# One pair more between the mix and the turn of a talking-heads attention: counting of sides, exp and selection two groups later, with nine score buffers

## What is computed

```python
q, k = l2norm(x @ Wq), l2norm(x @ Wk)            # 16 heads of 64; 4 memory keys ahead of k
dots = einsum('bhid,bhjd->bhij', q, k) * 10
dots = einsum('hg,bgij->bhij', W_pre_th, dots)   # heads are mixed
dots = where(causal, mask_value, dots)
vk   = top_k(dots, 64)[..., -1:]                 # the 64th largest of each row
attn = softmax(where(dots < vk, mask_value, dots))
attn = einsum('hg,bgij->bhij', W_post_th, attn)  # heads are mixed again
out  = einsum('bhij,bhjd->bhid', attn, v) * head_scale
out  = (out * sigmoid(x @ Wg + bg)) @ Wo
```

## Time and profile before

| | us |
|---|---|
| median of 3 runs | 2402.39 (2402.37 to 2406.88) |
| the profiled run | 2402.8 |
| its span, first to last instruction | 2401.0 |
| PE busy in the span | 2104.1 (88%) |
| DVE busy | 1801.4 (75%) |
| ACT busy | 1622.8 (68%) |
| POOL busy | 812.5 (34%) |

### The profile page before, as it was taken

One profiled execution on the slowest core, in us unless ns is written; L12 is line 12 of the kernel. 1 busy time (PEld: TensorE's weight loads), 2 busy tenths in 40 slices (PEclk: granted clock), 3 DMA queues, 4 the chain that ended last, 5 costly groups with the idle time before them and its releaser, 6 DMA issues. The chain is left out here.

```text
span 2401.0 us, 55203 instructions
## 1 busy us (share of the span) xinstructions
PE 2104.1 (88%) x16059; PEld 1363.1 (57%) x16060; DVE 1801.4 (75%) x7282; ACT 1622.8 (68%) x4700; POOL 812.5 (34%) x2274
## 2 busy tenths in 40 slices
PE   7995789898999998899989988998898889884997
PEld 3433456665566556665666666666666666563433
DVE  6564489868986898689868986898689868983446
ACT  4442578757876787678767885888588758871543
POOL 3001444344434433443344334433443344311000
PEclk9996899999999999999999999999999999997998
DMA  5002012101210121012101210121012101212001
GB/s 171 0 9 75 22 38 60 42 25 42 59 42 25 42 60 42 25 42 60 42 25 42 60 42 25 42 59 42 25 42 60 42 23 40 57 37 85 0 1 70
DMA packets 113218, 104.71 MB, mean 44 GB/s; under 512 B 34448, under 2 KB 110864, under 8 KB 112912
## 3 DMA queue, kind: packets, MB, share of 16 engines
q1 hardware_dynamic: 108000, 96.65, 15.8%
q10 hardware_dynamic: 4912, 4.46, 0.6%
HBM read 19.14 MB, written 12.71 MB: 13 GB/s over the span
## 5 line engine op out<-in xcount | busy, mean ns | idle before, releaser
L1491 DVE TENSOR_SCALAR_CACHE_REDUCE S<-S,minus_thr 128x68 f32<-128x68 f32 (+56 forms) x456 | 218.0, 514 | 225.6 <-POOL minus_thr L1388 224.8
L1048 PE MATMUL bankC<-R,E 128*128 128x128 f32 x2560 | 349.9, 286 | 34.6 <-POOL R L1395 34.6
L1048 PEld LDWEIGHTS bankC<-R,E 128*128 128x128 f32 x2560 | 337.3, 201 | 70.7 <-POOL R L1395 36.7
L1032 PE MATMUL bankB<-raw,mixpre 128*128 128x76 f32 (+37 forms) x1024 | 357.8, 437 | 19.3 <-DMA raw<-SC 19.2
L1244 ACT ACTIVATE S<-bankB,aim_first 128x68 f32<-128x68 f32 (+56 forms) x456 | 231.2, 510 | 201.5 <-PE bankB L1032 199.7
L1379 POOL TENSOR_TENSOR S<-S,diagmask 128x8 f32<-128x8 f32 x512 | 108.6, 216 | 688.2 <-ACT S L1244 654.7
L1022 PE MATMUL bankD<-KT,QT 64*64 64x258 f32 (+7 forms) x2304 | 195.6, 409 | 94.2 <-ACT SC L1233 86.0
L1395 POOL TENSOR_SCALAR R<-mixpost,rinv 128x128 f32<-128x128 f32 x512 | 184.8, 374 | 180.1 <-DVE rinv L1555 179.7
L1551 DVE SCALAR_TENSOR_TENSOR E<-S,limit,E 128x68 f32<-128x68 f32 (+56 forms) x456 | 221.2, 521 | 30.4 <-DVE E L1551 0.3
L1270 ACT ACTIVATE E<-S,nmax 128x12 f32<-128x12 f32 (+56 forms) x512 | 233.2, 505 | 14.5 <-POOL nmax L1409 14.5
L1074 PEld LDWEIGHTS bankM<-PT,V 128*64 128x64 f32 x5120 | 183.9, 141 | 102.4 <-issue 85.9
(11 more groups left out here) (176 smaller groups left out, 3968.8 us busy)
## 6 DMA issues: line engine op xcount, KB each, us to landing
X_first<-in_L_attn_x_dram ACTq DMA_DIRECT2D x8, 512.0 KB, 9.6
x<-X_first SPq DMA_DIRECT2D x8, 512.0 KB, 2.9
xt<-x SPq DMA_DIRECT2D x32, 128.0 KB, 2.4
x<-xt SPq DMA_DIRECT2D x32, 128.0 KB, 2.5
X_last<-x SPq DMA_DIRECT2D x8, 512.0 KB, 6.6
out_dram<-X_last SPq DMA_DIRECT2D x8, 512.0 KB, 2.8
raw<-SC SPq DMA_DIRECT2D x8, 258.0 KB, 3.0
raw<-SC SPq DMA_DIRECT2D x8, 254.0 KB, 3.5
```

What stands on the lines that cost most here:

```text
L1032: last = nc.tensor.matmul(bankB[n % 2][:, 0:wide(n)], W.mixpre[:, :], raw[n % RAWS][:, 0:wide(n)], start=True, stop=True)
L1048: last = nc.tensor.matmul(bankC[n % 2][:, jb * P:(jb + 1) * P], E[n % EBUFS][:, jb * P:(jb + 1) * P], R[n % RBUFS][:, :], start=True, stop ...
L1491: nc.vector.tensor_scalar(row, row, minus_thr[:, col(n)], None, ALU.add, ALU.max, accum_out=rmax[:, col(n)]).then_inc(max_done, 1)
```

## The change

The pipeline becomes one pair longer. `LAG` goes from 6 to 8, so turn and out_PT of a group lie eight groups behind its mix. count_sides and exp come four groups behind it instead of two, nmax and the clearing of E likewise, R six instead of four. select_pair keeps its loop variable, but row_max of n0+4 and n0+5 now stands at its end, where row_max of n0+2 and n0+3 stood ahead of it. gate_half, squares and residual come at a g that is 2 smaller in DVE's loop; ln_stats and ln_apply stay at theirs. There are nine buffers S instead of eight. EBUFS, RBUFS, RAWS and RING stay.

```diff
--- before.py
+++ after.py
@@ -21,7 +21,7 @@
 HD = H * DH
 J = N + MEM
 HALF = P // 2
-SBUFS = 8
+SBUFS = 9
 EBUFS = 6
 RBUFS = 4
 XBUFS = 6
@@ -30,7 +30,7 @@
 GATES_AT = (6, 6, 6, 6)
 V0_AT = 4
 V1_AT = 2
-LAG = 6
+LAG = 8
 RAWS = 6
 RING = 16
 REDO_SBUFS = 6
@@ -1316,9 +1316,9 @@
                     evict(n0 + 1)
                 for n in ranked_in(n0):
                     count_below(n)
-                for n in ranked_in(n0 - 2):
+                for n in ranked_in(n0 - 4):
                     count_sides(n)
-                for n in (n0 - 2, n0 - 1):
+                for n in (n0 - 4, n0 - 3):
                     if 0 <= n < NG:
                         exp(n)
                 if n0 >= LAG:
@@ -1403,8 +1403,8 @@
             for n0 in range(0, NG + LAG, 2):
                 t, g = divmod(n0, GPT)
                 live, ahead = n0 < NG, t + 1 < NT
-                if 0 <= n0 - 2 < NG:
-                    m = n0 - 2
+                if 0 <= n0 - 4 < NG:
+                    m = n0 - 4
                     pool.wait_ge(max_done, m + 2)
                     nc.gpsimd.tensor_scalar(nmax[:, ring((m, m + 1))], rmax[:, ring((m, m + 1))], -1.0, 1.0, ALU.mult,
                                             ALU.mult).then_inc(nmax_ready, 2)
@@ -1413,10 +1413,10 @@
                     mask(n0 + 1)
                 if ranked_in(n0):
                     threshold(ranked_in(n0))
-                for n in (n0 - 4, n0 - 3):
+                for n in (n0 - 6, n0 - 5):
                     if 0 <= n < NG:
                         scaled_mix(n)
-                for m in (n0 - 2, n0 - 1):
+                for m in (n0 - 4, n0 - 3):
                     if 0 <= m < NG and m % GPB < EBUFS:
                         if m >= EBUFS:
                             pool.wait_ge(turned, m - EBUFS + 1)
@@ -1553,6 +1553,9 @@
                         op0=ALU.is_ge, op1=ALU.mult, accum_out=rsum[:, col(n)]))
                 dve.wait_ge(tk, at[n0 + 1])
                 nc.vector.reciprocal(rinv[:, ring(both)], rsum[:, ring(both)]).then_inc(E_ready, 2)
+                if n0 + 4 < NG:
+                    row_max(n0 + 4)
+                    row_max(n0 + 5)
 
             def mark_batch(i):
 
@@ -1578,21 +1581,18 @@
             squares(1, 1)
             for n0 in range(0, NG, 2):
                 t, g = divmod(n0, GPT)
-                if 2 <= n0 and n0 + 2 < NG:
-                    row_max(n0 + 2)
-                    row_max(n0 + 3)
                 if g == 2 and t + 2 < NT:
                     ln_stats(t + 2)
                 select_pair(n0)
                 if g == 6 and t + 2 < NT:
                     ln_apply(t + 2)
-                if g % 8 == 2 and t:
+                if g % 8 == 0 and t:
                     gate_half(2 * t - 2 + g // 8)
-                if g == 14 and t + 2 < NT:
+                if g == 12 and t + 2 < NT:
                     squares(t + 2, 0)
-                if g == 6 and t >= 2:
+                if g == 4 and t >= 2:
                     residual(t - 2)
-                if g == 2 and t and t + 1 < NT:
+                if g == 0 and t and t + 1 < NT:
                     squares(t + 1, 1)
                 if (n0 + 2) % GPB == 0:
                     mark_batch(n0 // GPB)
```

## The result

| | before | after |
|---|---|---|
| median, us | 2403.53 (4 runs, 2402.37 to 2406.88) | 2416.75 (4 runs, 2414.60 to 2420.31) |
| ratio | | 1.0051, 95% interval 1.0031 to 1.0072 |
| profiled run, span | 2402.8, 2401.0 | 2417.8, 2416.0 |

Beside a later set of experiments the same kernel came out at 2421.58, ratio 1.0077 (1.0063 to 1.0091). The forecast was 2441: right in sign, inside its range, but its +38 was 13 to 18.

The account below looks back on a forecast made before the run. PE's queue was taken as the bound. Boundary +36.4, clock +11, turns -10.8, batch 0 -5.3 and drain +7.0 summed to +38 on 2402.8, giving 2441 us (56%), range 2407 to 2456.

Parts of the forecast that it names:

- What bounds the kernel, distances: Whole kernel: PE's queue sets the period; exp to turn stays four groups, so DVE's slack for a select grows no longer.
- DVE's chain, POOL's chain, PE at the boundary: Batch start: pair 508 ends at 1218.6, norm(t+1,0) at 1225.3, k transposes start at 1233.3, +5.2 us a boundary.
- q's transposes at 1229: Batch start on PE: q's transposes wait for the gates until about 1229, hidden ahead of k's at 1233.3.
- rise to 65 us: Sign of being right: PE's wait for qk rises from 30.7 to about 65 us.
- Boundary path (+36.4): Seven batch boundaries: k transposes start 5.2 us later at each, as norm(t+1,0) stands behind R of pair 508; +36.4 us.
- clock (+11): Batch boundaries: PE's longer wait brings one further clock dip, 1.5 to 1.7 us each; +11 us, other end 0.
- The step that failed: Inside a batch: nothing changes; DVE's shifted jobs cost nothing against PE, ln_stats and ln_apply 0.4 us in the chain.
- Turns (-10.8): PE, eight batches: each of three steps up in turn width comes one pair later, 1.35 us less a batch; -10.8 us.
- Drain (+7.0): Kernel's end: DVE has one more wide select after the last mix, R of pair 508 released later; +7.0 us.
- Batch 0 (-5.3): First batch: POOL's 5.30 us wait of R(0) for DVE leaves the path to PE's k transposes; -5.3 us.
- Ninth buffer: ScalarE's evict at a batch's end: deadline met with under 1 us to spare; costed at nothing, other end 1 us a batch.
- The rule weighed: Norm beside a selecting DVE: exclusion would cost 1.5 us a boundary, near 2451; left out, as norms spread only 112 ns.

Follow-up runs that it names:

- e3: Kernel before with only PE's turn and ScalarE's out_PT one pair later (LAG 8, seven E, five R); 2390.18 us, ratio 0.9926.
- e5: Changed kernel with POOL's norm(t+1,0), norm(t+1,1) and halo copy ahead of R and E's clearing, only in each batch's first tile; 2376.65 us, ratio 0.9883.
- e9: Changed kernel with only norm(t+1,0) ahead of R, only in the first tile of each batch; 2375.94 us, ratio 0.9892.
- e4: Kernel before with DVE's squares(t+1,1) directly behind select_pair, ahead of gate_half, and ln_stats last in the iteration; 2390.17 us, ratio 0.9931.
- e7: Changed kernel with eight score buffers S instead of nine; 2407.87 us, ratio 1.0025.
- e10: e5 with eight score buffers S instead of nine; 2414.71 us, ratio 1.0045.
- e12: Changed kernel unedited, measured again beside later runs; 2421.58 us, ratio 1.0077 to the kernel before.

## Why the prediction was right in kind and wrong in size

- **What bounds the kernel, distances:** held. PE's queue sets the period, and exp to turn is four groups in both. e3 shows the reverse: with that distance at six groups the turns' waits for R go, though 2.67 us a batch for ScalarE's copy come in their place.
- **DVE's chain, POOL's chain, PE at the boundary:** held closely. Counted from the batch's first eviction, the forecast put the end of pair 508 at 25.3 us, norm(t+1,0) at 32.0, ScalarE's exp at 32.1 and the k transposes at 40.0. Measured: 25.6 (1211.95), 32.2 (1218.53), 32.4 (1218.73), 39.6 (1225.94). The +5.2 was +4.9 (34.7 before). e5 and e9 show the cause: take norm(t+1,0) out of R's shadow and 5.6 us a boundary go.
- **A step with the right end and a wrong part:** I put q's transposes at 1229, hidden ahead of k's. They were the longer wait on PE, 2.74 us for the gates against 1.11 for qk; the wait list therefore showed no rise to 65 us, though PE lost what I had said.
- **Boundary path (+36.4) and clock (+11):** +39.5 in all. The path was mis-sized because I read one boundary of seven: in after the k transposes start 39.5 to 39.6 us after every batch's start, but in before 34.7 to 34.9 only in batches 2 to 6, and 36.3 and 36.6 in batches 1 and 7, where the granted clock was 0.50 in the first 6 us and not 0.72. So the path cost 29.9. The clock came as forecast: from the transposes to group 12 another 1.5 to 1.7 us in each of batches 2 to 7, none in batch 1, 9.5 in all.
- **The step that failed:** "Inside a batch, neighbours are equal but for 16 columns and nothing changes", and with it, "gate_half, squares and residual move one pair earlier in DVE's own count and so keep their place against PE; ln_stats and ln_apply come one job later, 0.4 us in the chain". I costed the new order of these jobs at nothing, and looked for what hangs on it only at the boundary. In tile 1 the k transposes had waited 1.39 to 1.42 us for norm(t+1,1), eight of the 26 waits that the earlier trace rows counts. In after that wait is gone in six batches and 0.2 to 0.3 us in two: -14.1 us over eight batches, the largest part of the miss. From DVE's first instruction behind its wait to the end of squares it takes 6.57 us in after (1267.97 to 1274.54) and took 8.85 in before (1267.23 to 1276.08). Of these 2.3 us, 0.8 are the statistics, which now stand behind squares. The other 1.5 are one DVE instruction that in before stood still until POOL's product of the q half ended, and in after ran before that product began. The rows, before and then after:

```profile
1267.23 0.39 DVE L1491 TENSOR_SCALAR_CACHE_REDUCE S<-S,minus_thr 128x172 f32<-128x172 f32 x1 [4.58 <-POOL minus_thr L1388]
...
1270.72 1.90 POOL L1373 TENSOR_TENSOR qk<-qk,rn 128x1024 f32<-128x1024 f32 x1
...
1270.96 1.69 DVE L1534 SCALAR_TENSOR_TENSOR picked<-iotaM,order,top 128x16 f32<-128x16 f32 x1
...
1272.59 0.23 DVE L1534 SCALAR_TENSOR_TENSOR picked<-iotaM,order,top 128x16 f32<-128x16 f32 x1
```

```profile
1267.97 0.16 DVE L1504 SCALAR_TENSOR_TENSOR side<-signs,middle 128x2 f32<-128x2 f32 x1 [4.56 <-ACT junk_side L1262]
...
1270.25 0.21 DVE L1534 SCALAR_TENSOR_TENSOR picked<-iotaM,order,top 128x16 f32<-128x16 f32 x1
...
1271.60 1.90 POOL L1373 TENSOR_TENSOR qk<-qk,rn 128x1024 f32<-128x1024 f32 x1
...
1273.12 1.21 DVE L1466 TENSOR_REDUCE ssq<-qksq 128x16 f32<-128x1024 f32 x1
...
1274.37 0.17 DVE L1467 TENSOR_SCALAR ssq<-ssq 128x16 f32<-128x16 f32 x1
```

e4 shows that the wait hangs on when squares end: it takes 1.4 us from the same chain by order alone and gains the same in the same groups. e3, with the turn's later width and the old order on DVE, keeps the wait (1.79), so the width is not the cause. No run separates the 0.8 from the 1.5. In tile 2 the wait rose from 0.33 to 1.25 us in the boundary's batch: +6.6 over eight. There the same kind of DVE instruction took 1.90 us (at 1322.34) where it had taken 0.79 (at 1325.01); no run isolates that. I had read only one of those 26 waits.
- **Turns (-10.8):** -9.5 in their groups. **Drain (+7.0):** +6.1; from the last eviction to DVE's last reciprocal it is 31.3 us, where it was 23.8.
- **Batch 0 (-5.3):** -7.8; norm(1,0) started at 256.48, ahead of the first R at 262.26, where R had waited until 263.17 with norm behind it. Of the rest, 4.4 us in its tile 1 are the step above.
- **The rest,** -5.7 over all other groups, partly stretches at the lower clock near groups 16 to 20 that came or went, is not settled by a run.
- **Ninth buffer "at nothing, with 1 us a batch as its other end":** in after it is worth less than nothing (e7), and in e5 it is worth 38 us (e10). Its price is not its own; it depends on what else waits for the same pair.
- **The rule weighed:** the 112 ns were no evidence. They are the spread of the power (L1369), with which DVE does not collide; it collides with the product (L1373), and there it is DVE that stands still while the product keeps its 1.90 to 1.93 us. In before this happened 32 times to the first L1534 of a pair (two inputs in SBUF): each lasted until the product's end, 0.51 to 1.96 us where 0.23 is usual, 34.5 us in all, the 1.5 us of tile 1 above among them. At the boundary read in e9 the price is one instruction (the next one of its kind took 0.22):

```profile
1192.42 0.41 DVE L1537 SCALAR_TENSOR_TENSOR picked<-iotaM,order,top 128x16 f32<-128x16 f32 x1
```

It ended with the product. By the rule of the Trainium skill ("SBUF — State Buffer", section "Who interferes with whom") the two exclude each other; the trace agrees for the product, at a price of 0.2 us in this boundary, 0.5 in four others and 1.1 in two, and not the 1.5 that I had worked out from it. It does not agree for the power (L1369, 2.92 us, which reads SBUF too): beside it DVE's instructions with two SBUF inputs were as short as ever, 46 of L1504 in before, 31 of L1534 and 12 of L1551 in after.

## What to carry to other kernels

Where several waits hang on one late event, taking away or adding one of them says nothing of the others: a buffer can be worth nothing with one order and 38 us with another, so move first what stands in the shadow of the event without needing it. A change that also shifts small jobs within an engine's iteration has to be costed at each place where someone waits for such a job; "26 times" in a list of waits means reading one of each kind, not the one beside the main change, and a boundary that is multiplied by seven should be read more than once. An instruction that lasts seven times as long as the next of its kind is a wait that no list of waits shows: here DVE's beside POOL's product. And lengthen only the distance that has too little slack (here exp to turn), not every stage together.

## What the runs showed of the hardware

A wait of PE does not by its length alone tell what the clock does. Before, a wait of 2.98 us was followed by a granted clock of 0.64; in after, one of 2.67 us in the same place was followed by 1.00 (window 1186 to 1190), and waits of 2.74 and 1.11 us with short work between them by 0.66 and 0.50. The same program also differs from run to run: in the drain of after and of e12, the same kernel, the windows from 2140 to 2200 us show 0.89 and 0.74, and the last projections begin 7.7 us apart (2193.56 and 2201.26), though the last evictions lie within 0.3 us:

```profile
2140.00:2200.00 60.00, 43.75 (x470) 35.10 (x470) 40.02 (x133) 23.14 (x55) 6.13 (x21) 0.89 0.03 8
```

```profile
2140.00:2200.00 60.00, 47.10 (x450) 38.42 (x449) 38.82 (x129) 22.86 (x54) 6.13 (x21) 0.74 0.01 4
```
